# Decoder layer: cross attention's outputs by transfers instead of turns, cross values on ScalarE, an interleaved middle chain, ends by sequence

## The reference

```python
x = x + self_attention(layernorm(x))       # latent q (64) and kv (32), 16 query heads, 4 kv heads, rope, causal
x = x + cross_attention(layernorm(x), ctx) # 16 heads of 16, biases bq, bk, bv, bo, mask over (query, key)
x = x + ffn(layernorm(x))                  # relu(x w1 + b1) rounded to fp8, w2 and b2 rounded, out rounded to fp16

# cross attention, per head
scores = jnp.where(mask == 0, -1e9, q @ k.T / 4)
out = softmax(scores) @ v                  # heads side by side, then @ wo.T + bo
```

## Time and profile before

| | |
|---|---|
| three runs | 1822.35, 1814.67, 1822.03 us, median 1822.03 |
| profiled execution | 1819.02 us, span of its instructions 1817.0 us |
| busy share | TensorE 92%, VectorE 69%, ScalarE 61%, GpSimd 40% |
| chain that ended last | TensorE 68%, VectorE 10%, issue 7%, ScalarE 5%, GpSimd 4%, DMA 3% |
| mean granted clock | 0.981 of 2.4 GHz |

### The profile page before, as it was taken

The page is one execution under the profiler, slowest core; times in us unless marked ns, Lnnn a source line. Parts: engine busy times, 40 slices in busy tenths (PEclk is TensorE's granted clock), DMA queues, the critical chain, the costliest instruction groups (busy, mean ns, idle before and its releaser), DMA issues.

```text
span 1817.0 us, 34264 instructions
## 1 busy us (share of the span) xinstructions
PE 1673.7 (92%) x12274; PEld 1015.8 (56%) x12274; DVE 1245.2 (69%) x1908; ACT 1103.6 (61%) x1704; POOL 724.2 (40%) x962
## 2 busy tenths in 40 slices
PE   3779999999999999999999999999999999999987
PEld 1445556556555565555556555665655556555554
DVE  4567486785848768586776848678585876858582
ACT  3355675756667565665756567575666756566572
POOL 3251353624435352433634345362443535243310
PEclk9979999999999999999999999999999999999998
DMA  6452552715346251633724255271534625163320
GB/s 170 59 83 39 76 88 36 122 28 85 57 64 100 36 95 38 92 67 43 121 36 79 49 75 88 36 119 30 84 59 62 101 36 95 37 93 57 48 37 12
DMA packets 86606, 124.07 MB, mean 68 GB/s; under 512 B 10481, under 2 KB 53938, under 8 KB 86322
## 3 DMA queue, kind: packets, MB, share of 16 engines
q1 hardware_dynamic: 83650, 115.26, 41.5%
q0 software_dynamic: 2160, 7.87, 1.2%
q10 hardware_dynamic: 768, 0.57, 0.1%
HBM read 21.42 MB, written 8.39 MB: 16 GB/s over the span
## 4 chain that ended last, share of the span: by engine, by line
PE 68%; DVE 10%; issue 7%; ACT 5%; POOL 4%; DMA 3%; SPq 2%; ACTq 0%; POOLq 0%
PE o_pair L1318 12%; PE small L1404 8%; PE small L1149 7%; DVE negmax L900 6%; PE score L1279 6%; PE o_pair L1149 3%; PE small L1331 3%; PE small L1165 3%; PE score L1256 3%; DMA Q<-negT 2%; PE small L1435 2%; PE score L1202 2%; DVE P L922 2%; PE score L1261 2%; ACT P L691 2%
## 5 line engine op out<-in xcount | busy, mean ns | idle before, releaser
L691 ACT ACTIVATE P<-score 128x1024 f32<-128x1024 f32 x448 | 446.8, 1026 | 119.7 <-PE score L1279 42.7
L900 DVE TENSOR_REDUCE negmax<-score 128x4 f32<-128x1024 f32 (+1 forms) x384 | 460.0, 1219 | 32.6 <-PE score L1237 19.8
L922 DVE TENSOR_TENSOR P<-P,cross_bound 128x1024 f32<-128x1024 f32 x192 | 255.6, 1365 | 65.8 <-ACT P L691 65.6
L1318 PE MATMUL o_pair<-P,V 128*32 128x256 f32 (+1 forms) x4096 | 283.1, 363 | 15.6 <-DVE P L922 15.6
L737 ACT ACTIVATE score<-cross_q 128x1024 f32<-128x1024 bf16 x192 | 196.5, 1023 | 60.3 <-DVE negmax L900 58.7
L468 POOL TENSOR_TENSOR negrest<-negmax,negparts 128x32 f32<-128x32 f32 x64 | 15.5, 243 | 502.1 <-ACT negparts L652 501.6
L1318 PEld LDWEIGHTS o_pair<-P,V 128*32 128x32 f32 x4096 | 86.2, 108 | 148.2 <-issue 78.1
L1279 PE MATMUL score<-Q,K 99*128 99x256 bf16 x1024 | 151.5, 275 | 13.3 <-DMA Q<-negT 12.2
L1435 PE MATMUL small<-xnT,w 128*128 128x256 f32 x600 | 156.7, 379 | 0.0
L1237 PE MATMUL score<-K,Q 96*128 96x256 bf16 x768 | 119.5, 279 | 33.8 <-ACT score L737 30.8
L1279 PEld LDWEIGHTS score<-Q,K 99*128 99x128 bf16 x1024 | 85.8, 98 | 100.8 <-issue 66.1
(11 more groups left out here) (181 smaller groups left out, 3219.4 us busy)
## 6 DMA issues: line engine op xcount, KB each, us to landing
Q<-q1p SPq DMA_DIRECT2D x96, 256.0 KB, 5.9
K<-k2p SPq DMA_DIRECT2D x96, 256.0 KB, 8.4
Q<-q2p SPq DMA_DIRECT2D x192, 128.0 KB, 4.0
x_in<-in_x SPq DMA_DIRECT2D x16, 512.0 KB, 5.6
ctxT<-in_ctx SPq DMA_DIRECT2D x16, 512.0 KB, 4.4
k2f<-q1f SPq DMA_DIRECT2D x32, 256.0 KB, 5.3
out_y<-x POOLq DMA_DIRECT2D x15, 512.0 KB, 3.6
K<-k1p SPq DMA_DIRECT2D x96, 64.0 KB, 4.5
```

What stands on the lines that cost most here:

```text
L691: A.activation(P[:, t % 4, :], score[b][:, :, :], ACT.Exp, scale=SCALE).then_inc(score_free[b], 1)
L900: V.tensor_reduce(negmax[:, k, h:h + 1024 // w], s.rearrange("p (h w) -> p h w", w=w), AX.X, ALU.max, negate=True).then_inc(score_free[b], 1)
L922: V.tensor_tensor(p, p, cross_bound[:, t % 2, :].unsqueeze(1).broadcast_to([128, 4, SEQ]), ALU.min).then_inc(probs_masked[1], 1)
L1318: last = T.matmul(o_ps[ob][32 * j:32 * j + 32, SEQ * gg + q0:SEQ * gg + SEQ], v, p, start=s == 0, stop=end, tile_position=(0, 32 * j), ski ...
```

## The change

Cross attention's outputs of groups 0 to 14 are no longer turned. V2 is laid out with values and ones in turn, so `o_pair` holds a value in every even partition and a sum in every odd one. From `o_sb`, SP sends per unit the 64 even partitions straight to `inT` (features on partitions; the weights `wo` are permuted on the host to that order, `by_unit`) and four rows of sums to `sums2`. VectorE inverts all sums of a group in one instruction of 32 x 256, SP spreads the inverses over 16 partitions a head by four transfers, and GpSimd multiplies. Only the last group is still turned.

ScalarE evacuates the cross values, without a bias; bv @ wo is added to bo once in the prologue. The second half of the keys is split by ScalarE and GpSimd instead of VectorE. GpSimd holds its ffn addition back until VectorE has taken the next group's first row maxima. In the middle chain, q1, k1, v1 and the hidden tiles h1, h2 are interleaved. SP sends the first maxima of the cross attention ahead of k1's parts. The prologue loads mask, b2 and w2 first and makes q1 of one sequence before the other; the end runs by sequence.

```diff
 # SP
+            def put_outputs2(g, u):
+                bank, before = o_bank(1, g, u)
+                b, gp = u // 2, u % 2
+                sp.wait_ge(o_free[bank], before + 1)
+                sp.dma_start(inT[64 * gp:64 * gp + 64, :, SEQ * b:SEQ * b + SEQ],
+                             o_sb[0:128:2, u % 2, :].rearrange("p (c q) -> p c q", c=NC)).then_inc(o2_moved[u % 2], 16)
+                sp.dma_start(sums2[8 * u:8 * u + 8, :], o_sb[1:128:32, u % 2, :]).then_inc(o2_moved[u % 2], 16)
+            def put_inverses2(g):
+                sp.wait_ge(inverse2_ready, g + 1)
+                for b in range(GB):
+                    for c in range(NC):
+                        sp.dma_start(over_sum[:, c, SEQ * b:SEQ * b + SEQ],
+                                     inverse2[16 * b + c:16 * b + 16:2, :].unsqueeze(1).broadcast_to([8, HD, SEQ])
+                                     ).then_inc(inverse2_moved[b], 16)
                 if prev:
                     put_neg(st, 1, 1)
-                for b in range(GB):
-                    put_neg(st, 0, b)
-                for n in range(3):
+                    for u in range(UNITS):
+                        put_outputs2(i - 1, u)
+                    put_inverses2(i - 1)
+                put_neg(st, 0, 0)
+                for n in range(2):
                     put_part("k2", n, i)
+                put_neg(st, 0, 1)
+                put_part("k2", 2, i)
...
+                put_neg(st, 1, 0)
+                if nxt:
                     put_part("k1", 0, i + 1)
-                put_neg(st, 1, 0)
 # GpSimd
+            def over_sums(g, b):
+                for n in range(2):
+                    pool.wait_ge(o2_moved[n], 32 * (UNITS // 2) * (g + 1))
+                pool.wait_ge(inverse2_moved[b], 16 * NC * (g + 1))
+                at = slice(SEQ * b, SEQ * b + SEQ)
+                G.tensor_tensor(inT[:, :, at], inT[:, :, at], over_sum[:, :, at], ALU.mult).then_inc(o2_whole, 1)
+            def keys_rest(st, g):
+                pool.wait_ge(small_free[st.bank("k2_1")], st.this("k2_1"))
+                G.tensor_tensor(k2f[:, 1, :], k2f[:, 1, :], k2p[:, 0, 1, :], ALU.subtract).then_inc(rest1["k2"], 1)
+                keys_rest(st, i)
                 if prev:
+                    for b in range(GB):
+                        over_sums(i - 1, b)
                     add_bias2(i - 1)
                 cut_rest(0, i, 1)
...
                 if prev:
+                    if nxt:
+                        n, before = tile("S1", i + 1, 0)
+                        pool.wait_ge(score_free[n], before + 1)
                     add_ffn(st, i - 1)
 # ScalarE
+            def keys_full(st, c):
+                bk = st.bank(f"k2_{c}")
+                A.activation(k2f[:, c, :], small[bk][:, :], ACT.Identity, bias=bk2[:, c:c + 1]).then_inc(small_free[bk], 1)
+            def values2(st, r):
+                bk = st.bank(f"v2_{r}")
+                act.wait_ge(small_full[bk], st.this(f"v2_{r}"))
+                A.activation(V2[:, 2 * r:2 * r + 2, :, 0:32:2],
+                             small[bk][:, :].rearrange("p (k h n) -> p k h n", k=2, n=HD), ACT.Copy).then_inc(small_free[bk], 1)
+                    if t == 1 and a == 0:
+                        values2(st, 1)
+                values2(st, 0)
                 cut_first(0, i, 0)
...
-                if prev:
-                    turns(st, "oT2_", inT)
 # VectorE, in body
                 for t in range(N1):
                     row_max(0, i, t)
-                    if prev and t in (1, 4):
-                        normalise(st, 1, 2 if t == 1 else 3, i - 1)
+                    if prev and t == 3:
+                        for n in range(2):
+                            dve.wait_ge(o2_moved[n], 32 * (UNITS // 2) * i)
+                        V.reciprocal(inverse2[:, :], sums2[:, :]).then_inc(inverse2_ready, 1)
...
-                    if t == 5:
-                        values2(st, 0)
-                    if t == 7:
-                        keys_rest(st, i, 1)
 # TensorE, in body
-                if prev:
-                    unit_turn(st, 1, i - 1, 3)
...
-                if prev:
-                    heads_turned(st, 1)
...
-                    copied(st, "oT2_")
                     for r in range(2):
+                        pe.wait_ge(o2_whole, GB * (i - 1) + r + 1)
                         tokens(st, "out2", inT, wo2, r)
...
-                    for c in range(NC):
-                        query1(st, c)
+                    query1(st, 0)
+                if prev:
+                    hidden_half(st, 1, 0)
+                if nxt:
+                    query1(st, 1)
+                if prev:
+                    hidden_half(st, 1, 1)
+                if nxt:
                     key1(st)
+                if prev:
+                    hidden_half(st, 2, 0)
+                    hidden_half(st, 2, 1)
+                pe.wait_ge(xn_ready[1], GB * i + 2)
+                turned_batch(st, "xnT2_1", 1, xn)
+                if nxt:
                     for r in range(2):
                         value1(st, r)
 # TensorE, the end (the hidden tiles of one sequence, then the other)
+            batch_copied(END, "oT2_0")
+            tokens(END, "out2", inT, wo2, 0)
+            unit_turn(END, 1, NG - 1, 3)
...
+            turned_batch(END, "xnT3_0", 0, xn)
...
+            tokens(END, "out2", inT, wo2, 1)
+            end_hidden(0)
...
+            ffn_out(END, 0)
+            end_hidden(1)
+            ffn_out(END, 1)
```

More of the change, by code:

```diff
@@ L680, in unit_out @@
                     act.wait_ge(pv_done, g * PVS + PV0[a] + (u + 1) * TPU[a])
-                    if u >= 2:
+                    if u >= 2 and a == 1 and not last:
+                        act.wait_ge(o2_moved[u % 2], 32 * (g * (UNITS // 2) + u // 2))
+                    elif u >= 2:
                         name = f"o{a + 1}t{u - 2}"
@@ L972, in query2_third @@
                 V.tensor_tensor(q2p[:, 2, b], q2f[:, b], q2p[:, 1, b], ALU.subtract).then_inc(part3["q2"], 1)
-            def values2(st, r):
-                bk = st.bank(f"v2_{r}")
-                dve.wait_ge(small_full[bk], st.this(f"v2_{r}"))
-                bank, free = small[bk], small_free[bk]
-                for k in range(2):
-                    last = V.tensor_tensor(V2[:, 2 * r + k, :, 0:HD],
-                                           bank[:, 256 * k:256 * k + 256].rearrange("p (h n) -> p h n", n=HD),
-                                           bv2[:, :].rearrange("p (h n) -> p h n", n=HD), ALU.add)
-                last.then_inc(free, 1)
             dve.wait_ge(x_loaded, 16)
@@ L1022, in _ @@
             V.tensor_copy(cross_bound[:, :, :], bank[:, :].rearrange("p (k q) -> p k q", k=2)).then_inc(free, 1)
+            dve.wait_ge(loaded, 16 * LOADS)
+            bk = PRO.bank("bias")
+            dve.wait_ge(small_full[bk], PRO.this("bias"))
+            V.tensor_tensor(bo2[:, :], small[bk][:, 0:DM], bo2[:, :], ALU.add).then_inc(small_free[bk], 1)
+            dve.wait_ge(part1["q1"], 1)
+            V.tensor_tensor(q[1], q[1], q1p[:, 0, :, SEQ:TOK], ALU.subtract).then_inc(rest1["q1"], 1)
+            dve.wait_ge(part2["q1"], 1)
+            V.tensor_tensor(q1p[:, 2, :, SEQ:TOK], q[1], q1p[:, 1, :, SEQ:TOK], ALU.subtract).then_inc(part3["q1"], 1)
             def cross_bounds(st, g, i=None, nxt=False):
@@ L1467, in _ @@
                 value1(PRO, r)
-            pe.wait_ge(loaded, 16 * LOADS)
             bk = PRO.bank("maskT")
@@ L1483, in _ @@
             last.then_inc(filled, 1)
+            bk = PRO.bank("bias")
+            pe.wait_ge(small_free[bk], PRO.before("bias"))
+            pe.wait_ge(loaded, 16 * LOADS)
+            for c in range(NC):
+                last = T.matmul(small[bk][:, 0:DM], bv2[:, c:c + 1].broadcast_to([128, 128]), wo2[:, c, :],
+                                start=c == 0, stop=c == NC - 1)
+            last.then_inc(small_full[bk], 1)
             def body(i, prev, nxt):
@@ L1601, in _ @@
-            pe.wait_ge(small_free[END.bank("oT2_1")], END.this("oT2_1"))
-            tokens(END, "out2", inT, wo2, 1)
-            pe.wait_ge(xn_ready[2], NG)
-            for c in range(NC):
-                turned(END, f"xnT3_{c}", xn, c)
-            copied(END, "xnT3_")
-            hidden(END, range(HT))
-            pe.wait_ge(small_free[END.bank(f"h{HT - 1}")], END.this(f"h{HT - 1}"))
-            for r in range(2):
-                ffn_out(END, r)
+            attend(END, 1, NG - 1, "last")
@@ new lines, in end_hidden @@
+            def end_hidden(b):
+                at = slice(SEQ * b, SEQ * b + SEQ)
+                for j in range(HT // 2):
+                    bk = END.bank(f"h{b}_{j}")
+                    pe.wait_ge(small_free[bk], END.before(f"h{b}_{j}"))
+                    bank, filled = small[bk], small_full[bk]
+                    for n in range(2):
+                        t = 2 * j + n
+                        for c in range(NC):
```

(14 more changed lines are left out.)

295 lines of the change are left out of this document (182 added, 113 removed).

## The result

The changed kernel takes 1886.7 us (median of 4 runs, 1881.7 to 1888.3) against 1822.2 before: ratio 1.036, 95% interval 1.032 to 1.039. It is 145 us above the forecast of 1742, slower than before where faster was forecast, and not in the way of any rival.

A forecast was written before the change was run, and what follows sets the result against it. TensorE was taken to hold most of the chain. Savings of 33 (parts 1 and 2) + 13.6 + 12 + 10 + 8 = 76.6 us took the span from 1817.0 to 1740.4, forecast 1742 us; range 1715 to 1780.

The forecast's parts named there:

- part 5: SP's order: first cross maxima ahead of k1 saves 12 us; keys ahead of second self maxima costs nothing.
- Part 1: Cross exponents: unit turns and a 0.92 us wait go, 2.4 us by the second self tile, stage about 19.4.
- part 2: Self maxima: 20.5 us; transfer lands in 4.0, VectorE stands 1.5, reciprocal 0.5, bias costs TensorE 0.3 per iteration.
- near 103.5: The period of one loop iteration, in us, that the new profile was expected to show.
- rival C: Output transfers land early, within 2.5 us, and VectorE does not stand: 1720 us; chance 0.16.
- Part 3: Cross values copied by ScalarE, 0.6 us more in each of two stages: costs nothing, at most 9 us.
- Part 4: Middle chain: reordered matmuls remove the clock falls behind the run of short ones, 13.6 us saved.
- Rival A: The clock falls stay despite the reordered middle chain: 1756 us; chance 0.15.
- Part 6: The ends: first score 10 us earlier (7 to 13), and 8 us saved at the end.
- Rival D: Two output and inverse transfers in series decide, 8.4 us each, slower: about 1850 us; chance 0.08.
- Rivals B and E: B: output transfers land late, 5.9 us, 1775; E: ScalarE or VectorE binds the cross exponents, 1757; together 0.13.

The follow-up runs named there:

- Experiment 1: The changed kernel with SP sending both sequences' self maxima ahead of all parts of the cross keys: 1808.0 us, ratio 0.993 to the kernel before.
- experiment 2: Experiment 1's kernel with the load of the next x (x_in, 512 KB) issued behind the second cross maxima: 1781.1 us, ratio 0.978.
- experiment 11: Experiment 2's kernel with the last parts of q1 and k1 sent behind the second cross maxima and x_in's load: 1767.0 us, ratio 0.972.
- experiment 12: Experiment 11's kernel with the output bias at the head of GpSimd's list for the self maxima: 1760.8 us, ratio 0.969.
- experiment 4: The kernel before with only the new order of the middle chain on TensorE and ScalarE: 1804.9 us, ratio 0.992.
- experiment 7: Experiment 2's kernel with the middle chain in the old order (q1, q1, k1, v1, then hidden tiles): 1789.6 us, ratio 0.984.
- experiment 10: The kernel before with only the first sequence's cross maxima sent ahead of k1's first part: 1823.0 us, ratio 1.003.
- experiment 5: The changed kernel with only the second sequence's self maxima sent by ScalarE, keys still ahead in SP's list: 1882.2 us, ratio 1.035.

## Why the prediction was wrong

The step that failed is in part 5: "The keys' five transfers now go before the second of these; it may land 1 us late with some slack, I cost it at nothing". I read the issue times in the queue and gave the small transfer a duration of its own. It has none: with 1.28 MB ahead it lands when they have landed, 6.6 us after its issue, 3.1 after TensorE asks, and the half clock behind the wait adds 2.5. The rows had the sign of it: 256 KB of keys, in a run of six, took 8.4 us to land, and 256 KB of q1 5.9. Experiment 1 puts 79 us on it, more than half of the miss.

The next 41 us are the same mechanism in the cross exponents (27 for x_in, experiment 2; 14 for the last parts, experiment 11). That order was in the kernel before too, at no cost. There the second cross maxima were issued 5.6 us after the stage's start, as after (5.7), and TensorE used them without a wait:

```profile
580.42 0.61 PE L1279 MATMUL score<-Q,K 99*128 99x256 bf16 x4
```

That is 10.6 us after the start. In the changed kernel TensorE asks at 9.7, since VectorE's stall is gone, and they are usable at 11.8. So 0.9 us of the wait are the earlier demand, and at least 1.2 a later landing. The last part of k1 leaves 0.7 us later in the stage there (2.3 against 1.6 us after its start): the wait at the stage's head has shrunk from 0.93 to 0.26 us, and GpSimd's split of k1 hasn't moved. Whether that is all of the delay was not tested. Part 1 asked which engine would take over at 19.4 and found none; it did not ask which landing.

The last 6 us down to the fastest variant are GpSimd's bias (experiment 12); part 2 had 0.3 us an iteration for it in the sum. 1886.7 - 79 - 27 - 14 - 6 = 1761, and 19 us stay between that and the forecast. By the sum a loop iteration without a fall should go from 106.8 to 103.8 (the "near 103.5" isn't the sum's), and it lasts 104.4: 7 us in thirteen iterations. They are part 5's: third and fourth stage together last 64.7, as before (64.65), though the wait for the first cross maxima fell to 0.27. TensorE waits 1.13 us for ScalarE's mask there, 0.35 in experiment 4. The first iteration is 5.5 us over (TensorE waits 2.3 us for VectorE in its self maxima, and the clock falls), the last one, the start and the end together 6.5.

The parts, one by one:

- **Part 1** (19.4 us): right in size, 19.38 once no landing is in the way; 21.6 to 23.2 in the changed kernel.
- **Part 2** (self maxima 20.5): right, 20.33, by two errors that cancel, which is luck. VectorE waits 0.47 us for the sums, not 1.5: the last 128 KB of outputs and 8 KB of sums are both there 2.9 and 2.3 us after their issues (lines below), between rival C's 2.5 and the 4.0 of the sum, and VectorE still stood a little. (The 2.3 us estimated beside rival C came from a section on transfers that GpSimd issues; these are SP's.) The reciprocal takes 1.74 us, not 0.5. Against 16 elements at 253 ns that is (1741 - 253) / 240 = 6.2 ns an element. The Trainium skill's rule ("VectorE: DVE Perf Modes", "First, the fixed hardware budget"), read as 2 us, was the nearer; VectorE stands and divides for 2.2 us, 2.0 in the forecast.
- **Part 3** (0): no wait for the copy was seen; it was not tried by itself.
- **Part 4** (13.6): right, 14.6 in experiment 4, all falls of the loop gone. Rival A falls with experiments 4 and 7. In the changed kernel's variants the same order is worth 8.5, most of it in three iterations with two falls; a single fall costs 1.8 us an iteration before and nothing there (experiment 7). The rule named with rival A (the Trainium skill, "TensorE: Matmul & The Clock Gate", "HAM oscillation — how this bites in real kernels") fits the fall behind the 3.1 us wait, not those behind a busy TensorE, which the order of the matmuls removed.
- **Part 5** (12): wrong by itself, nothing or 5 us slower in experiment 10. The wait's length was taken as its worth.
- **Part 6** (10 and 8): 11.3 for the first score (40.7 us; 41.2 to 43.3 in the variants, and 50.2 to 50.6 instead of 52.0 in those of the kernel before), 5.3 for the end.
- **Rival D** had the right sign and an outcome of 1850, but by the outputs' transfers; TensorE never waited for these. Rivals B and E did not come either.

The lines for part 2, SP's queue and VectorE in the changed kernel:

```profile
839.71 0.62 SPq L389 DMA_DIRECT2D inT<-o_sb  x1
840.38 0.56 SPq L391 DMA_DIRECT2D sums<-o_sb  x1
```
```profile
842.65 1.74 DVE L1190 RECIPROCAL inverse<-sums 32x256 f32<-32x256 f32 x1 [0.47 <-DMA sums<-o_sb]
```

Why a transfer completes behind the others is the rule of the Trainium skill named in experiment 5; the runs show that the queue makes no difference and the amount ahead does. How a wait of some us turns into half clock was not varied by itself: behind the 3.1 us the clock fell in every iteration, behind the 2.3 us of experiment 5 in twelve of fifteen.

## What to carry to other kernels

In this kernel a small transfer costs what is in flight ahead of it, from whatever queue. For each one that an engine waits for, add up the bytes issued shortly before it (here within 10 us), at the rate of the trace (here some 120 GB/s for the keys), and put bulk with slack behind it; its slack is to be read anew whenever the waiting engine gets faster. A wait that the profile shows is worth its length only if nothing else is about as late: look at the waits around it before you book it. The same holds for a fall of the clock.

## What the runs showed of the hardware

- 24 KB took 6.6 us to their use from SP's queue and 6.55 from ScalarE's with 1.28 MB of keys ahead, 9.3 with three keys (0.77 MB) just before and two just behind, and at most 3.45 with no keys ahead and six behind (experiment 1); the 8 KB of sums, issued behind 128 KB, were in use after 2.3 us.
- A wait of 3.1 us of TensorE was followed by 6.05 us with a mean clock of 0.54 of 2.4 GHz; behind waits of 2.1 to 2.3 us the clock fell in some iterations and in others not (the third stage of experiment 5: 46.7 or 44.0 us). It also fell to 0.50 with TensorE busy 4.00 of 4.00 us before, and with the products in the new order it did not, in the loop.
- VectorE's reciprocal takes 1741 ns for 256 elements a partition, 253 for 16.
- An addition of GpSimd over 128 x 1024 takes 3.1 us beside VectorE's bound and 2.1 beside its row maxima; the bound takes 2.8 instead of 1.25 beside it.
